# A fused attention and feed-forward kernel: the sixteen value products of a quad of heads issued in one block instead of two halves

## The chip, the cores and the metric

The kernel runs on one core of one Trainium2 chip. The metric is the device time of one execution in microseconds (us). The core has a matrix engine (TensorE, in the profile PE, with its weight loads as PEld), VectorE (DVE), ScalarE (ACT), GpSimd (POOL) and SyncE (SP), which issues DMAs. Each engine runs its own instructions in the order in which they are written; semaphores tie the engines to each other. Matrix products land in PSUM, which has eight banks of 128 x 512 f32.

## The reference, cut to what matters

```python
x = L0_attn_x                                    # (16, 512, 128) f32
x = x + _layernorm(attention(_layernorm(x)))     # 16 heads of width 8, queries serve as keys
x = x + _layernorm(feed_forward(_layernorm(x)))

# attention
q = (x @ Wq.T + bq).reshape(B, S, 16, 8)
v = (x @ Wv.T + bv).reshape(B, S, 16, 8)
bits = (einsum('bshe,en->bshn', concat(q, 1), hyperplanes) >= 0)   # 6 bits: 64 buckets
same = bucket[:, :, :, None] == bucket[:, :, None, :]
scores = einsum('bhsd,bhtd->bhst', q, q) / sqrt(128)
attn = softmax(scores * (62 + same), axis=-1)
out = einsum('bhst,bhtd->bhsd', attn, v)

# feed_forward, ternary weights with a scale for each output
h = silu(lin(x, w1)) * lin(x, w2)                # 128 -> 512
h = gelu(lin(h, h1)); h = gelu(lin(h, h2))       # 512 -> 512 -> 512
return lin(h, w3)                                # 512 -> 128
```

## The kernel before, in words

The sixteen sequences are sixteen iterations (called batches here). The work of one batch is spread over several of them: while iteration i computes the attention scores of batch i, it also does the feed-forward layers of batch i - 1, the last steps of batch i - 2, and the projections of the batches to come. The first two iterations have less of that, the last two as well, and a finale written out by hand ends the program.

**Tiles.** A batch has 64 score tiles: tile k is head k // 4 and rows 128 (k % 4) to 128 (k % 4) + 127. For each tile TensorE makes one bf16 matmul of 128 x 512 into one of four PSUM banks (`scores`, L593; tile k uses bank k % 4). It waits until tile k - 4 has been taken from that bank. VectorE (`attend_tile`, from L926) waits for the scores of tile k, then makes the coefficients 62 or 63 of tile k + 1 (`coefficients`, L901), and then in one instruction multiplies tile k by its coefficients, writes the logits to SBUF and takes the row maxima (L951). So the wait for scores k stands ahead of the coefficients of tile k + 1. The logits lie in a ring of 48 tiles.

**Groups and quads.** Eight tiles (two heads) are a group. Their maxima are transposed by VectorE, sent to DRAM and read back broadcast to all partitions (max_row); GpSimd then subtracts (L1125, two instructions for each group) and ScalarE exponentiates (`exponential`, L1185, 128 x 1024 each, eight for each quad). Sixteen tiles (four heads) are a quad. Its value products (`weigh_values`, L615) are sixteen matmuls, each of a stationary operand of 128 x 32 (values and a column of ones, padded) and a moving operand of 128 x 512. The four heads of the quad use four column strips of the array and four partition strips of one bank, aux_bank; j counts the four blocks of 128 keys. Two quads make a pair: their products accumulate in aux_bank, ScalarE copies them (oT, L1206), TensorE transposes them back (L624), ScalarE inverts the sums (rden, L1216), and VectorE divides (att, L974).

**What sets the order.** There is no scheduler. An iteration has 256 steps, four for each tile, and tables of numbers say after which step a piece of work is written out on its engine: scores k stand at step 4k, ahead of everything else of that step. `PV_SLOTS` has the steps of the sixteen value products j = 0..3 of quads 0 to 3 (each number stands for the four matmuls of one j); a number over 256 means the next iteration. In the program of before, j = 0 and 1 stand at one step and j = 2 and 3 at a later one, with one or two scores in between. The first half waits until all but two of the exponentials of the quad are done (probs_done), the second half waits for the last two. Feed-forward matmuls (L711 and L725 the gate and up products, L739 and L750 the two hidden layers, L766 the output) stand at steps of their own in between. The up products share banks with earlier ones: the third of them waits for VectorE's second multiply (L1007). On ScalarE, feed-forward activations, normalisations (L1321 is that of the attention output, which waits for a bias that VectorE makes) and exponentials alternate in a fixed order.

**Names used below.** L593 scores; L615 value products; L624 transposes of the output; L901 coefficients; L951 logits and maxima; L974 division; L1007 multiply of gate and up; L1185 exponentials; L1206 copy oT; L1216 rden; L1321 normalisation of the attention output.

Of the kernel before, what the change touches and what calls it, by code (L numbers as in the profile page):

```python
# [78 lines left out]
OUTPUT_BANK = 2  # L79


PV_SLOTS = (140, 140, 144, 144, 208, 208, 216, 216, 272, 272, 280, 280, 336, 336, 344, 344)
COPY_SLOTS = (218, 345)
TRANSPOSE_SLOTS = (231, 353)
SUM_SLOTS = (225, 363)
# [74 lines left out]
def sandwich_kernel(nc, x, wqT, bq, wvT, bv, hyper_blocks, hyper_bias, w1T, w2T, h1T, h2T, scales, w3T, w3_s, out):  # L160
    ctx = ExitStack()
    with ctx:
# [216 lines left out]
        def batches_at(i, k, slot, attend, feed):  # L379

            if attend and k == slot:
                return [i]
            if feed and k == slot - STEPS:
                return [i - 1]
            return []
# [189 lines left out]
        def _(pe):  # L575
# [20 lines left out]
            def weigh_values(b, quad, j, query, project):  # L596

                if j == 0:
                    if quad == 0:
                        pe.wait_ge(v_added, b + 1)  # L600

                    if quad == 0 and project:
                        pe.wait_ge(v_added, b + 2)
                    elif quad == 2 and query:
                        pe.wait_ge(q_part_steps, 4 * (b + 3))
                    elif quad % 2 == 0 and (begun(b) or quad):
                        pe.wait_ge(att_done, b * PAIRS + quad // 2)

                    pe.wait_ge(probs_done, b * (TILES // 2) + (quad + 1) * QT // 2 - GROUP)
                if j == 2:  # L610
                    pe.wait_ge(probs_done, b * (TILES // 2) + (quad + 1) * QT // 2)
                values = v_pad[:, b % 2].rearrange("p r n -> p (r n)")
                for hh in range(4):
                    first = 2 * PAD_PITCH * j + (PAD_PITCH - HALF_W) * (quad % 2) + VW * (quad // 2 * 4 + hh)
                    last = nc.tensor.matmul(aux_bank[hh * VW:(hh + 1) * VW, :], values[:, first:first + VW],  # L615
                                            logits[:, ring(b, quad * QT + hh * ST + j), :], start=(j == 0 and quad % 2 == 0),
                                            stop=(j == ST - 1 and quad % 2 == 1))
                if j == ST - 1:
                    last.then_inc(pv_psum, 1)
# [152 lines left out]
            def iteration(i, query, project, attend, feed, finish):  # L772
# [7 lines left out]
                for k in range(STEPS):  # L780
# [3 lines left out]
                    for quad in range(QUADS):  # L784
                        for j in range(ST):
                            for b in batches_at(i, k, PV_SLOTS[quad * ST + j], attend, feed):
                                weigh_values(b, quad, j, query, project)
# [708 lines left out]
```

## Time and profile before

| | us |
|---|---|
| median of 3 runs | 1331.74 |
| lowest and highest | 1331.31 to 1335.26 |
| the profiled execution, its own time | 1333.48 |
| its span, from the first to the last instruction | 1331.7 |
| busy in the span: TensorE | 1223.8 |
| busy: VectorE | 1212.8 |
| busy: ScalarE | 1091.9 |
| busy: GpSimd | 1167.6 |

An engine's busy time is the time in which one of its instructions runs. In the timeline a row is an instruction or several merged ones, with start and duration; the idle time ahead of it and what ended that stand in brackets. Each f32 matmul is two instructions of TensorE in the trace, so a half quad is sixteen rows of L615 and a quad thirty-two. Matmuls overlap: the next may start before the one before has ended.

### The profile page before, as it was taken

The numbers are of one execution on the slowest core, as the hardware profiler recorded it, in microseconds if no ns is written. First come the engines' busy times: TensorE is split into PE (matmuls) and PEld (weight loads), VectorE is DVE, ScalarE is ACT, GpSimd is POOL, SyncE is SP. The second block draws the span as 40 slices with busy tenths as digits, with TensorE's granted clock in tenths as the row PEclk, the third lists the DMA queues.
The fourth block names the chain that finished last, engine by engine and source line by source line (L and its number), as shares of the span: only waits on it lengthen the run. The fifth ranks groups of instructions, "written<-read, shape, count | busy, mean of one in ns | idle before, by whom it ended". The sixth has DMA issues, their size and how long they took to land. (4 is left out here: it accounts for less than half of the span.)

```text
span 1331.7 us, 19972 instructions
## 1 busy us (share of the span) xinstructions
PE 1223.8 (92%) x5406; PEld 506.8 (38%) x5406; DVE 1212.8 (91%) x3800; ACT 1091.9 (82%) x1693; POOL 1167.6 (88%) x304
## 2 busy tenths in 40 slices
PE   4667799999999999999999999999999999999998
PEld 1211244334344434434343433434343443434344
DVE  4989999999999999999999999999999999999920
ACT  2255879979798998989798897979889897988964
POOL 2599999999999999999999999999999999999600
PEclk9777999999999999999999999999999999999999
DMA  3474445435444543545454445544444454455200
GB/s 90 143 207 121 128 126 144 125 105 160 132 138 119 154 125 99 158 133 154 116 148 132 121 130 140 144 125 134 132 128 122 140 144 126 125 140 124 72 1 16
DMA packets 89237, 167.13 MB, mean 126 GB/s; under 512 B 18082, under 2 KB 54052, under 8 KB 89124
## 3 DMA queue, kind: packets, MB, share of 16 engines
q1 hardware_dynamic: 89016, 165.56, 45.1%
q8 instruction: 43, 0.70, 0.2%
q14 instruction: 70, 0.57, 0.1%
q10 hardware_dynamic: 108, 0.30, 0.1%
HBM read 150.33 MB, written 15.47 MB: 125 GB/s over the span
## 5 line engine op out<-in xcount | busy, mean ns | idle before, releaser
L1125 POOL TENSOR_TENSOR logits<-max_row,logits 128x2048 f32<-128x2048 f32 x252 | 1139.2, 4560 | 72.9 <-DMA max_row<-max_scratch 72.5
L951 DVE CUSTOM_DVE_ANT_0 logits<-s_bank,coeff 128x512 f32<-128x512 f32 x1024 | 691.6, 676 | 0.0
L1185 ACT ACTIVATE logits<-logits 128x1024 f32<-128x1024 f32 x504 | 503.0, 1047 | 92.6 <-POOL logits L1125 92.1
L901 DVE TENSOR_SCALAR coeff<-brow,bcol 128x516 bf16<-128x516 bf16 x1024 | 486.0, 475 | 29.2 <-PE s_bank L593 27.3
L593 PE MATMUL s_bank<-mov_stack,stat_stack 128*128 128x512 bf16 x1024 | 346.3, 393 | 46.4 <-DVE rowmax L951 40.4
L615 PE MATMUL aux_bank<-logits,v_pad 128*32 128x512 f32 x2016 | 247.3, 609 | 12.5 <-ACT logits L1185 12.4
L750 PE MATMUL f_bank<-hid_b,h_sb 128*128 128x512 f32 x480 | 236.7, 595 | 0.9 <-ACT hid_b L1355 0.9
L739 PE MATMUL f_bank<-hid_a,h_sb 128*128 128x512 f32 x480 | 234.4, 592 | 0.0
L593 PEld LDWEIGHTS s_bank<-mov_stack,stat_stack 128*128 128x128 bf16 x1024 | 95.6, 98 | 340.1 <-DVE rowmax L951 206.1
L739 PEld LDWEIGHTS f_bank<-hid_a,h_sb 128*128 128x128 f32 x480 | 90.2, 190 | 72.7 <-issue 61.8
L750 PEld LDWEIGHTS f_bank<-hid_b,h_sb 128*128 128x128 f32 x480 | 88.7, 190 | 66.3 <-issue 54.9
L615 PEld LDWEIGHTS aux_bank<-logits,v_pad 128*32 128x32 f32 x2016 | 53.3, 110 | 148.7 <-issue 114.5
L951 DVE DVE_READ_ACCUMULATOR2_ANT rowmax<- 128x1 f32 x1024 | 83.7, 82 | 0.0
L711 PE MATMUL f_bank<-ynT,w_sb 128*128 128x512 f32 x120 | 62.2, 620 | 10.6 <-ACT hid_a L1349 5.1
L1355 ACT ACTIVATE hid_b<-f_bank,scales_sb 128x512 f32<-128x512 f32 x60 | 38.0, 684 | 33.6 <-PE f_bank L739 33.4
L766 PEld LDWEIGHTS f_bank<-w_sb,hid_a 128*128 128x128 f32 x480 | 59.2, 192 | 16.2 <-issue 12.2
L725 PE MATMUL f_bank<-ynT,w_sb 128*128 128x512 f32 x120 | 64.4, 618 | 0.0
L1132 POOL TENSOR_TENSOR ffn<-ffn,y 128x512 f32<-128x512 f32 x15 | 19.1, 1275 | 49.3 <-ACT ffn L1198 49.3
L766 PE MATMUL f_bank<-w_sb,hid_a 128*128 128x128 f32 x480 | 62.0, 278 | 0.0
L1007 DVE SCALAR_TENSOR_TENSOR hid_a<-f_bank,scales_sb,hid_a 128x512 f32<-128x512 f32 x60 | 44.7, 746 | 4.6 <-PE f_bank L725 4.6
L1349 ACT ACTIVATE hid_a<-f_bank,scales_sb 128x512 f32<-128x512 f32 x60 | 37.9, 684 | 2.1 <-PE f_bank L711 1.8
L1355 ACT ACT_TABLE_LOAD x30 | 38.5, 1283 | 0.5
(168 smaller groups left out, 994.9 us busy)
## 6 DMA issues: line engine op xcount, KB each, us to landing
max_row<-max_scratch SPq DMA_DIRECT2D x128, 512.0 KB, 3.9
brow<-bucket_scratch SPq DMA_DIRECT2D x63, 522.0 KB, 6.3
mov_stack<-q_scratch SPq DMA_DIRECT2D x192, 96.0 KB
stat_stack<-q_scratch SPq DMA_DIRECT2D x189, 96.0 KB
max_scratch<-rowmax_T SPq DMA_DIRECT2D x512, 1.0 KB
q_scratch<-q_parts SPq DMA_DIRECT2D x16, 384.0 KB, 4.7
x_in<-in_x SPq DMA_DIRECT2D x16, 256.0 KB, 3.0
q_scratch<-q_parts SPq DMA_DIRECT2D x16, 256.0 KB, 5.2
```

Of the source, the lines that this page charges most:

```text
L593: nc.tensor.matmul(tile_bank(k)[:], stat_stack[:, quad % 2, hh, t * P:(t + 1) * P], mov_stack[:, quad % 2, hh, :], start=True, stop=True). ...
L615: last = nc.tensor.matmul(aux_bank[hh * VW:(hh + 1) * VW, :], values[:, first:first + VW], logits[:, ring(b, quad * QT + hh * ST + j), :], ...
L711: nc.tensor.matmul(f_bank[GATE_BANKS[j]][:], w1_sb[:, col], ynT[:], start=True, stop=True).then_inc(w1_psum, 1)
L725: nc.tensor.matmul(f_bank[UP_BANKS[j]][:], w2_sb[:, col], ynT[:], start=True, stop=True).then_inc(w2_psum, 1)
L739: last = nc.tensor.matmul(f_bank[FIRST_HIDDEN_BANKS[j]][:], h1_sb[:, k, col], hid_a[:, k, :], start=(k == 0), stop=(k == HT - 1))
L750: last = nc.tensor.matmul(f_bank[SECOND_HIDDEN_BANKS[j]][:], h2_sb[:, k, col], hid_b[:, k, :], start=(k == 0), stop=(k == HT - 1))
L766: last = nc.tensor.matmul(f_bank[OUTPUT_BANK][:, t * P:(t + 1) * P], hid_a[:, j, t * P:(t + 1) * P], w3_sb[:, j, :], start=(j == 0), stop= ...
L901: nc.vector.tensor_scalar(coeff[:, k % 3, :].rearrange("p (r n) -> p r n", r=ROW_RUNS), brow[:, h // 4 % 2, h % 4, :, 0:RUN], bcol[:, b % ...
L951: nc.vector.tensor_tensor_reduce(out=logits[:, ring(b, k), :], in0=tile_bank(k)[:], in1=coeff[:, k % 3, 0:SEQ], scale=float(E) ** -0.5, sc ...
L1125: nc.gpsimd.tensor_tensor(tiles[:, :, t:t + 2], max_row[:, m % 2].unsqueeze(2).broadcast_to([P, GROUP, 2, SEQ]), tiles[:, :, t:t + 2], ALU ...
L1185: nc.scalar.activation(logits[:, first:first + 2, :], logits[:, first:first + 2, :], ACT.Exp, scale=-1.0).then_inc(probs_done, 1)
L1355: nc.scalar.activation(hid_b[:, j, :], f_bank[FIRST_HIDDEN_BANKS[j]][:], ACT.Gelu, scale=scales_sb[:, 2, j:j + 1]).then_inc(h1_done, 1)
```

## The change

Of the table of steps for the value products, sixteen numbers are replaced. Of quad 0, j = 2 and 3 move from step 144 to 140, so they follow j = 0 and 1 directly. Of the other three quads, the first half moves four steps (one tile) later and the second half four steps earlier: 208 and 216 become 212, 272 and 280 become 276, 336 and 344 become 340. The waits stay in front of the same products: the wait for the quad's last two exponentials stands ahead of j = 2, now inside the block. The orders of VectorE, ScalarE, GpSimd and SyncE are unchanged. Quads 2 and 3 of the last batch are written out by the finale and are as before.

```diff
-PV_SLOTS = (140, 140, 144, 144, 208, 208, 216, 216, 272, 272, 280, 280, 336, 336, 344, 344)
+PV_SLOTS = (140, 140, 140, 140, 212, 212, 212, 212, 276, 276, 276, 276, 340, 340, 340, 340)
```

TensorE, quad 3 of the batch before (steps 80 to 92 of an iteration; quad 2, steps 16 to 28, reads the same). s_bank0 takes scores 20, s_bank1 scores 21, s_bank2 scores 22, s_bank3 scores 23; x8 and x16 count products:

```order
 L750 MATMUL f_bank2<-hid_b,h2_sb 128x512 x2
 L593 MATMUL s_bank0<-mov_stack,stat_stack 128x512
-L615 MATMUL aux_bank<-logits,v_pad 32x512 x8
-L593 MATMUL s_bank1<-mov_stack,stat_stack 128x512
-L593 MATMUL s_bank2<-mov_stack,stat_stack 128x512
-L615 MATMUL aux_bank<-logits,v_pad 32x512 x8
+L593 MATMUL s_bank1<-mov_stack,stat_stack 128x512
+L615 MATMUL aux_bank<-logits,v_pad 32x512 x16
+L593 MATMUL s_bank2<-mov_stack,stat_stack 128x512
 L593 MATMUL s_bank3<-mov_stack,stat_stack 128x512
 L593 MATMUL s_bank0<-mov_stack,stat_stack 128x512
```

Scores 21 moved ahead of the first eight products, and scores 22 stand behind all sixteen.

TensorE, quad 0 (steps 136 to 146); s_bank3 takes scores 35, s_bank0 scores 36, s_bank1 scores 37, and L766 is the feed-forward output:

```order
 L750 MATMUL f_bank1<-hid_b,h2_sb 128x512
 L593 MATMUL s_bank3<-mov_stack,stat_stack 128x512
-L615 MATMUL aux_bank<-logits,v_pad 32x512 x8
-L593 MATMUL s_bank0<-mov_stack,stat_stack 128x512
-L615 MATMUL aux_bank<-logits,v_pad 32x512 x8
+L615 MATMUL aux_bank<-logits,v_pad 32x512 x16
+L593 MATMUL s_bank0<-mov_stack,stat_stack 128x512
 L766 MATMUL f_bank2<-w3_sb,hid_a 128x128 x4
 L593 MATMUL s_bank1<-mov_stack,stat_stack 128x512
```

Scores 36 moved from between the halves to behind them.

TensorE, quad 1 (steps 208 to 216); s_bank0 takes scores 52, s_bank1 scores 53, s_bank2 scores 54, L725 are up products and L739 the first hidden layer:

```order
 L725 MATMUL f_bank1<-ynT,w2_sb 128x512
 L593 MATMUL s_bank0<-mov_stack,stat_stack 128x512
-L615 MATMUL aux_bank<-logits,v_pad 32x512 x8
-L725 MATMUL f_bank1<-ynT,w2_sb 128x512
-L593 MATMUL s_bank1<-mov_stack,stat_stack 128x512
-L593 MATMUL s_bank2<-mov_stack,stat_stack 128x512
-L615 MATMUL aux_bank<-logits,v_pad 32x512 x8
+L725 MATMUL f_bank1<-ynT,w2_sb 128x512
+L593 MATMUL s_bank1<-mov_stack,stat_stack 128x512
+L615 MATMUL aux_bank<-logits,v_pad 32x512 x16
+L593 MATMUL s_bank2<-mov_stack,stat_stack 128x512
 L725 MATMUL f_bank2<-ynT,w2_sb 128x512
```

The third up product and scores 53 moved ahead of the value products, scores 54 behind them all.

## Rows read from the trace of the kernel before

**Rows 1.** Page; stretch of batch 7: busy PE, PEld, DVE, ACT, POOL, clock.

```profile
PE 1223.8 (92%) x5406; PEld 506.8 (38%) x5406; DVE 1212.8 (91%) x3800; ACT 1091.9 (82%) x1693; POOL 1167.6 (88%) x304
...
567.60:644.20 76.60, 73.77 (x338) 31.21 (x337) 74.62 (x237) 68.62 (x107) 74.70 (x19) 1.00 0.49 134
```

**Rows 2.** VectorE's waits (total, times, longest): whole span, tiles 18-25 of batches 7, 10.

```profile
DVE coeff L901 <- PE s_bank L593: 27.3, 63, 4.7
...
DVE coeff L901 <- PE s_bank L593: 0.3, 1, 0.3
...
DVE coeff L901 <- PE s_bank L593: 1.4, 1, 1.4
```

**Rows 3.** Timeline (start, duration) of TensorE at quad 0's first half, batch 7.

```profile
603.67 0.38 PE L593 MATMUL s_bank<-mov_stack,stat_stack 128*128 128x512 bf16 x1
...
604.43 0.61 PE L615 MATMUL aux_bank<-logits,v_pad 128*32 128x512 f32 x4
...
605.29 0.61 PE L615 MATMUL aux_bank<-logits,v_pad 128*32 128x512 f32 x4
605.84 0.39 PE L593 MATMUL s_bank<-mov_stack,stat_stack 128*128 128x512 bf16 x1
```

**Rows 4.** Timeline of TensorE, then VectorE, at quad 2 (tiles 0 to 7).

```profile
568.58 0.38 PE L593 MATMUL s_bank<-mov_stack,stat_stack 128*128 128x512 bf16 x1
...
573.14 0.60 PE L593 MATMUL s_bank<-mov_stack,stat_stack 128*128 128x512 bf16 x2
...
568.54 0.68 DVE L951 CUSTOM_DVE_ANT_0 logits<-s_bank,coeff 128x512 f32<-128x512 f32 x1
...
573.15 0.48 DVE L901 TENSOR_SCALAR coeff<-brow,bcol 128x516 bf16<-128x516 bf16 x1
```

**Rows 5.** Timeline at quad 3: TensorE, VectorE; last, TensorE waiting at scores 45.

```profile
586.26 0.38 PE L593 MATMUL s_bank<-mov_stack,stat_stack 128*128 128x512 bf16 x1
...
593.41 0.38 PE L593 MATMUL s_bank<-mov_stack,stat_stack 128*128 128x512 bf16 x1
...
590.37 0.47 DVE L901 TENSOR_SCALAR coeff<-brow,bcol 128x516 bf16<-128x516 bf16 x1
...
593.83 0.48 DVE L901 TENSOR_SCALAR coeff<-brow,bcol 128x516 bf16<-128x516 bf16 x1 [0.28 <-PE s_bank L593]
...
615.46 0.39 PE L593 MATMUL s_bank<-mov_stack,stat_stack 128*128 128x512 bf16 x1 [0.54 <-DVE rowmax L951]
```

**Rows 6.** Timeline behind quad 3: TensorE in batch 2, ScalarE in batch 7.

```profile
206.95 0.66 PE L624 MATMUL aux_bank<-ident,oT 128*128 128x128 f32 x4 [0.54 <-ACT oT L1206]
...
590.95 0.58 ACT L1206 COPY oT<-aux_bank 128x512 f32<-128x512 f32 x1 [0.70 <-PE aux_bank L615]
```

**Rows 7.** Timeline at quad 0: VectorE's coefficients 37, ScalarE's last exponentials of the quad.

```profile
608.89 0.44 DVE L901 TENSOR_SCALAR coeff<-brow,bcol 128x516 bf16<-128x516 bf16 x1
...
603.34 2.00 ACT L1185 ACTIVATE logits<-logits 128x1024 f32<-128x1024 f32 x2
```

**Rows 8.** Timeline at quad 1: VectorE; last, where ScalarE's unbroken chain begins.

```profile
624.08 0.74 DVE L1007 SCALAR_TENSOR_TENSOR hid_a<-f_bank,scales_sb,hid_a 128x512 f32<-128x512 f32 x1
...
629.76 0.47 DVE L901 TENSOR_SCALAR coeff<-brow,bcol 128x516 bf16<-128x516 bf16 x1
...
631.22 0.75 DVE L1007 SCALAR_TENSOR_TENSOR hid_a<-f_bank,scales_sb,hid_a 128x512 f32<-128x512 f32 x1 [0.38 <-PE f_bank L725]
632.29 0.48 DVE L901 TENSOR_SCALAR coeff<-brow,bcol 128x516 bf16<-128x516 bf16 x1 [0.32 <-PE s_bank L593]
...
634.83 0.42 DVE L974 TENSOR_TENSOR att<-aux_bank,rden 128x256 f32<-128x256 f32 x1 [0.35 <-ACT rden L1216]
...
601.31 1.61 ACT L1321 ACTIVATE f_bank<-att,att_bias,att_rstd 128x128 f32<-128x128 f32 x4 [0.31 <-DVE att_bias L1019]
```

**Rows 9.** Batch 1 at quad 2: the view of stretches, then VectorE's timeline.

```profile
107.40:110.60 3.20, 3.20 (x18) 0.59 (x18) 3.20 (x11) 0.00 (x0) 3.20 (x1) 0.56 0.41 111
...
112.23 0.47 DVE L901 TENSOR_SCALAR coeff<-brow,bcol 128x516 bf16<-128x516 bf16 x1
```

## The prediction, made before the changed kernel ran

> **What bounds the kernel now.** I read the page first, then the windows of single batches, then who waits for whom, then the timeline of TensorE and VectorE side by side. Times in us are from the span's start; batch 7 (567.6 to 644.2) is my model batch, and "scores n" is the L593 matmul of tile n of a batch (64 tiles each). Over the span TensorE, VectorE and GpSimd are each busy for about nine tenths [rows 1]. Inside a batch of 76.6 VectorE works 74.6, GpSimd 74.7 and TensorE 73.8, at full granted clock [rows 1]. So VectorE is the bound, with about 2 us of holes per batch, and TensorE is close behind. The holes are named by the waits: 27.3 us in 63 waits of the coefficients L901 for scores, and in a batch the single wait at scores 25 is 0.3 at its shortest and 1.4 at its longest [rows 2]. (For the twelve like batches 2 to 13 it is 1.1, 1.1, 1.2, 0.4, 0.3, 0.3, 0.3, 0.3, 1.4, 0.3, 1.2, 0.7; two of these rows are shown.)
>
> What couples the two engines is four PSUM banks. Scores n may start when L951 has emptied tile n-4, which a wait of L593 on VectorE shows (the last row of [rows 5]), about 0.06 after; VectorE needs scores n before coefficients n+1. A bare VectorE tile is 1.00 us long (from L951 of tile 1 at 568.54 to the end of that of tile 5 at 573.15 are four tiles and one L951 of 0.61) [rows 4]. So TensorE has 3.0 us from "may start" to "is needed", and a TensorE block between two scores that is longer than that makes VectorE wait, unless VectorE has other work there.
>
> **The length of a block.** Each product is two f32 instructions, four products run side by side, and a group of four instructions follows the one before by 0.43 (604.43 to 605.29 is two groups) [rows 3]. A half quad (16 instructions) costs 2.17 from the scores ahead of it (603.67) to those behind it (605.84) [rows 3]. The whole quad is then 2.17 + 4 x 0.43 = 3.89. Two halves cost 4.34 and part a pair of scores; whole, the same work with one plain scores step (0.22, from the pair of L593 at 573.14 that takes 0.60, less 0.38 for one of them [rows 4]) is 4.11. So TensorE saves 0.23 per quad, what it costs to enter and leave the four-column form once. 62 quads are merged (the last two are issued by the finale): 14 us less TensorE time, but 3.89 is longer than 3.0. The DMAs, the other engines' orders and all durations stay.
>
> The Trainium skill (TensorEngine Tiling (Array Packing), Key Properties) says that changing the tiling mode drains TensorE. The rows bear this out in kind. By that rule alone the change is a plain gain of some 14 us; the coupling above is what speaks against it. The sum below does not use this.
>
> **Place A, quad 2 (scores 4 to 8).** Before, the first half follows scores 4 at 568.58 [rows 4] and fills the time until scores 5 may go. Now scores 5 come first: they wait for L951 of tile 1 (568.54 + 0.68 = 569.22) + 0.06 = 569.28, and TensorE stands idle for 0.5. Scores 6 start at 569.28 + 3.89 = 573.17, land at +0.39 = 573.56, and VectorE sees them at 573.60. It wants them at 573.15 [rows 4]. **VectorE +0.45**, TensorE +0.24 behind the block (scores 7 at 573.38 against 573.14). The scores behind it had little spare, but VectorE slips by more than TensorE, so nothing more is lost.
>
> **Place B, quad 3 (scores 20 to 25).** Scores 20 at 586.26 + 0.24 = 586.50 [rows 5]; scores 21 at 586.72 (VectorE's freeing is due at about the same time); scores 22 at 590.61, seen at 591.04. VectorE wants them at 590.37 + 0.45 = 590.82 [rows 5]: **+0.22**, together 0.67. TensorE is back on its old time (+0.24 - 0.23). Today VectorE waits 0.28 for scores 25 (593.41, used at 593.83) [rows 5]; arriving 0.67 later, it no longer does. **Net +0.39** in a batch whose wait there is 0.28. In general the slip is 0.67 less that wait, not below nothing. Where the wait is long it is not TensorE's own queue but L624 waiting for ScalarE's copy oT (206.95, idle 0.54) [rows 6], which hangs on GpSimd and stands still when VectorE slips. In batch 7 that copy waits for this block instead (590.95, 0.70) [rows 6] and comes 0.2 earlier, of no use.
>
> **Place C, quad 0 (scores 35 to 37).** Scores 36 move from 605.84 to 603.96 + 3.89 = 607.85 (scores 35 slip 0.29), seen at 608.28. VectorE wants them at 608.89 + 0.38, since statistics lie in between [rows 7]: **nothing**, the cover is 1.0.
>
> **Place D, quad 1 (scores 52 to 56).** Today TensorE waits 1.0 before the first half. Now L725 is ahead of it and waits as long for the multiply L1007 (624.08 + 0.74 = 624.82) [rows 8]. Scores 53 then at 624.88 + 0.86 = 625.74, in time (today VectorE waits 0.28 for them). Scores 54 at 629.63, seen at 630.06; wanted at 629.76 - 0.28 = 629.48: 0.58 late. The multiply that now waits 0.38 for L725 does not wait. Scores 55 at 629.63 + 0.22 + 1.72 = 631.57 (today 631.88), used at 631.99 against 632.29 [rows 8]: 0.3 gained. But next on VectorE is the division L974, which already waits 0.35 for ScalarE's rden (634.83) [rows 8]. ScalarE has no hole between L1321 (601.31, released by VectorE) and that rden [rows 8], and it has slipped with VectorE before. So the 0.3 becomes a longer wait at L974, about 0.65: **nothing kept**.
>
> **Sum of the twelve like batches.** 0.39 in the five whose wait is 0.3 (6, 7, 8, 9, 11), 0.3 in batch 5, nothing in 2, 3, 4, 10, 12, 13: 5 x 0.39 + 0.3 = **2.3**. Bounds: 0.39 less 12 x 0.3 if D's gain stays (-1.3), and 12 x 0.45 if GpSimd's lateness moves along with VectorE (+5.4).
>
> **Opening, batch 1.** Here TensorE is not loaded, starts A after an idle stretch, and the half quad runs at the lower clock level: 107.40 to 110.60 has a granted clock of 0.56 [rows 9], and TensorE is at the half quad for all of its 3.2. The whole quad behind scores 5 (108.06) then lasts about 5, scores 6 are seen at about 113.5 and wanted at 112.23 less today's 0.22 [rows 9]: +1.3. B likewise, estimated +0.9. At D (full clock) scores 54 and 55 come 0.55 and 0.28 late, where nothing is late today, and L974 does not wait: +0.8. Together **3.0**, between 0.9 (A and B at full clock) and 4.5. In batch 0 VectorE waits for ScalarE behind the blocks for longer than they cost: 0. **Batches 14 and 15** have less VectorE work beside the blocks (larger stalls in B) and get the waits of today back at scores 10, 23 and 25: between 0 and 0.8 each, I take 0.5: **1.0**.
>
> Sum: 2.3 + 3.0 + 1.0 = **+6.3**. The profiled execution took 1333.48 with a span of 1331.7; it lies 1.7 above the median of the runs, 1331.74. The sum would make it 1339.8, and the median 1331.74 + 6.3 = **1338.0**.
>
> **Rivals.** (1) The slips are swallowed. GpSimd is as full as VectorE [rows 1]; where its lateness sets scores 25 nothing is lost, and D's 0.3 may stay if ScalarE is early. 12 x 0.3 = 3.6 off the sum: 1334.4, within the noise. For it: half the batches show it now. Against: ScalarE's unbroken chain at D. Chance 0.25. (2) It is faster: what the denser products save TensorE is worth more than the long block costs. This holds if A and B don't stall, that is if a block really takes under 3.4 from scores to scores; then the waits at scores 25, 53, 55 and L1007 (0.28 + 0.28 + 0.32 + 0.38 = 1.26) fall by some half, 12 x 0.6 = 7 us: 1325. Against: 3.89 is counted from measured groups. Chance 0.09. The drain rule's own result, TensorE as the bound and 62 x 0.23 = 14 us less, gives 1317.5; VectorE's 74.6 of work per batch allows 2 us at most per batch, so chance 0.02. (3) Much slower: the wait for the quad's last exponentials now stands in mid-block with scores queued behind it. At C ScalarE is done at 603.34 + 2.00 [rows 7] + 0.38 = 605.72, and TensorE comes to the second half at 603.96 + 0.31 + 4 x 0.43 = 605.99, a margin of 0.3; the scores behind have 1.0 more, so it decides once ScalarE is over 1.3 late, or if at B GpSimd's late batches hold the block. At 0.5 per batch more: 12 x 0.5 on top, 1344. Chance 0.07. That the change does nothing is excluded by the order shown.
>
> **Numbers.** Forecast 0.57, rivals as above. A measurement tells about 0.3% (4.0 us) from no change, so slower begins at 1335.7. The forecast case falls below that bound at times (its own bounds reach from +1 to +11). Slower 0.61, same 0.28, faster 0.11. Range 1331 to 1343: it takes in rival 1 and most of the forecast's bounds.
>
> **What would show it.** L615 busy time falls by some 2 x 0.1 per quad. VectorE's waits on scores shift: none at 25 in most batches, new ones of 0.45 at scores 6, 0.2 at 22, 0.55 at 54, none at 53. TensorE gets a wait of 0.5 on VectorE before scores 5. L974's wait grows from 0.35 to about 0.65, sixteen times. Like batches are 77.0 or 77.5 long. If L974's wait does not grow, rival 1 is right; if scores 6 come in time, rival 2; a wait for exponentials inside L615 speaks for rival 3. The weakest terms are the opening and how GpSimd's lateness falls among the batches.

## The result, and the profile after

| | before | changed |
|---|---|---|
| median | 1331.74 | 1338.74 |
| lowest and highest | 1331.31 to 1335.26 | 1337.73 to 1340.93 |
| the profiled execution, its own time | 1333.48 | 1337.73 |
| its span | 1331.7 | 1335.9 |

The ratio is 1.0049, with a 95% interval of 1.0033 to 1.0066: the change makes the kernel slower, by 7 us in the medians. The medians are those of five runs of each. The profiled execution of the changed kernel is its fastest run, so the two profiles are only 4.2 us apart.

First the page of the changed kernel, the row that answers to [rows 1], and three of its groups (busy, mean ns of one, idle time ahead and what ended it):

```profile
PE 1215.8 (91%) x5406; PEld 516.6 (39%) x5406; DVE 1212.6 (91%) x3800; ACT 1091.3 (82%) x1693; POOL 1167.5 (87%) x304
...
L901 DVE TENSOR_SCALAR coeff<-brow,bcol 128x516 bf16<-128x516 bf16 x1024 | 486.7, 475 | 37.8 <-PE s_bank L593 35.7
...
L615 PE MATMUL aux_bank<-logits,v_pad 128*32 128x512 f32 x2016 | 234.8, 607 | 0.0
...
L725 PE MATMUL f_bank<-ynT,w_sb 128*128 128x512 f32 x120 | 62.8, 605 | 16.0 <-DVE hid_a L1007 16.0
```

TensorE is busy 8.0 us less (1223.8 in [rows 1]), and VectorE's waits for scores are 8.4 longer (27.3 in [rows 2], now 35.7). VectorE does the same work as before (1212.8 and 1212.6). TensorE's saving became idle time of TensorE and waiting time of VectorE.

Where in a batch this happens is shown by batch 7 of the changed kernel (572.1 to 649.0). Place A, TensorE, then VectorE; it answers to [rows 4]:

```profile
573.77 0.39 PE L593 MATMUL s_bank<-mov_stack,stat_stack 128*128 128x512 bf16 x1 [0.33 <-DVE rowmax L951]
574.09 3.64 PE L615 MATMUL aux_bank<-logits,v_pad 128*32 128x512 f32 x32
577.66 0.61 PE L593 MATMUL s_bank<-mov_stack,stat_stack 128*128 128x512 bf16 x2
...
577.63 0.08 DVE L951 DVE_READ_ACCUMULATOR2_ANT rowmax<- 128x1 f32 x1
578.09 0.48 DVE L901 TENSOR_SCALAR coeff<-brow,bcol 128x516 bf16<-128x516 bf16 x1 [0.38 <-PE s_bank L593]
```

TensorE waits for a bank ahead of scores 5, scores 6 start 3.89 us behind scores 5 (573.77 to 577.66), and VectorE, which has finished tile 5 at 577.71, waits 0.38. Place B and place D on VectorE, against [rows 5] and [rows 8]:

```profile
595.57 0.48 DVE L901 TENSOR_SCALAR coeff<-brow,bcol 128x516 bf16<-128x516 bf16 x1 [0.17 <-PE s_bank L593]
...
634.92 0.48 DVE L901 TENSOR_SCALAR coeff<-brow,bcol 128x516 bf16<-128x516 bf16 x1 [0.61 <-PE s_bank L593]
...
636.85 0.48 DVE L901 TENSOR_SCALAR coeff<-brow,bcol 128x516 bf16<-128x516 bf16 x1 [0.18 <-PE s_bank L593]
...
639.58 0.42 DVE L974 TENSOR_TENSOR att<-aux_bank,rden 128x256 f32<-128x256 f32 x1 [0.55 <-ACT rden L1216]
```

New waits stand at scores 22 and 54; that at scores 25 is gone, that at 55 is smaller, the multiply does not wait for L725, and the division waits 0.55 where it waited 0.35.

VectorE's waits, added up (total, times, longest), first in batch 1 and then in batches 2 to 13. Before:

```profile
DVE coeff L901 <- PE s_bank L593: 0.8, 3, 0.3
...
DVE coeff L901 <- PE s_bank L593: 18.0, 48, 1.4
DVE hid_a L1007 <- PE f_bank L725: 4.6, 12, 0.4
DVE att L974 <- ACT rden L1216: 4.2, 12, 0.4
```

After:

```profile
DVE coeff L901 <- PE s_bank L593: 5.1, 4, 2.4
...
DVE coeff L901 <- PE s_bank L593: 20.0, 63, 0.6
DVE att L974 <- ACT rden L1216: 6.7, 12, 0.6
```

In batches 2 to 13 the sum is the same in these two executions: 18.0 + 4.6 + 4.2 = 26.8 before, 20.0 + 6.7 = 26.7 after. In batch 1 it grew from 0.8 to 5.1. The batches' lengths say so too, taken from one L951 of tile 0 to the next (batch 15: to the end of its last L951): batch 1 75.3 and 80.1; batches 14 and 15 together 147.6 and 148.5; batches 2 to 13 together 924.9 and 924.6. But the last pair hides two movements. The shortest like batch grew from 76.63 to 76.91; and GpSimd's late batches, over 77.4 long and five of the twelve before, are one of twelve after.

What makes a batch late can be read from GpSimd's timeline. It is busy for 73.6 to 73.8 in every like batch of both kernels; what differs is when the DMA that brings the maxima back lets it go on, early in the batch. Batch 9 of before (from 720.9 on, 76.6 long) and batch 10 (from 797.5 on, 77.8 long):

```profile
727.69 4.54 POOL L1125 TENSOR_TENSOR logits<-max_row,logits 128x2048 f32<-128x2048 f32 x1 [1.34 <-DMA max_row<-max_scratch]
...
806.95 4.54 POOL L1125 TENSOR_TENSOR logits<-max_row,logits 128x2048 f32<-128x2048 f32 x1 [2.40 <-DMA max_row<-max_scratch]
```

It goes on 6.8 and 9.5 into the batch. Before, the batches in which this comes at 8.4 or earlier are 76.6 to 76.7 long, but for one of 77.6 in which a second wait for the same DMA follows; from 8.7 on they are 77.1 to 77.8. After, they are 76.9 up to 8.6, and 77.2 to 77.5 from 8.9 on. Four batches of before came later than 9.0 and none of after, so part of the second movement is how late this DMA was in each execution.

The end moved as well: from the last L951 to the end of the span it is 77.6 before and 76.7 after. In the traces of all kernels with quad 1 not in halves in the last batches it is 76.6 to 77.0, in all others 77.4 to 77.8.

### The profile page after: what moved, and what is told of

It reads as the page before. It is cut to its first block and busy times, and to the rows that moved or that the text cites. A ratio compares the mean times of both kernels' runs of the same rounds, so it can differ in the third digit from the quotient of the medians.

```text
span 1335.9 us, 19972 instructions
## 1 busy us (share of the span) xinstructions
PE 1215.8 (91%) x5406; PEld 516.6 (39%) x5406; DVE 1212.6 (91%) x3800; ACT 1091.3 (82%) x1693; POOL 1167.5 (87%) x304
## 5 line engine op out<-in xcount | busy, mean ns | idle before, releaser
L1125 POOL TENSOR_TENSOR logits<-max_row,logits 128x2048 f32<-128x2048 f32 x252 | 1139.1, 4553 | 77.1 <-DMA max_row<-max_scratch 73.7
L951 DVE CUSTOM_DVE_ANT_0 logits<-s_bank,coeff 128x512 f32<-128x512 f32 x1024 | 692.3, 676 | 0.0
L901 DVE TENSOR_SCALAR coeff<-brow,bcol 128x516 bf16<-128x516 bf16 x1024 | 486.7, 475 | 37.8 <-PE s_bank L593 35.7
L593 PE MATMUL s_bank<-mov_stack,stat_stack 128*128 128x512 bf16 x1024 | 350.0, 396 | 52.2 <-DVE rowmax L951 46.4
L615 PE MATMUL aux_bank<-logits,v_pad 128*32 128x512 f32 x2016 | 234.8, 607 | 0.0
L739 PE MATMUL f_bank<-hid_a,h_sb 128*128 128x512 f32 x480 | 234.4, 592 | 0.0
L593 PEld LDWEIGHTS s_bank<-mov_stack,stat_stack 128*128 128x128 bf16 x1024 | 98.3, 99 | 348.0 <-DVE rowmax L951 199.6
L739 PEld LDWEIGHTS f_bank<-hid_a,h_sb 128*128 128x128 f32 x480 | 90.2, 190 | 72.7 <-issue 61.7
L615 PEld LDWEIGHTS aux_bank<-logits,v_pad 128*32 128x32 f32 x2016 | 59.7, 111 | 146.7 <-issue 121.1
L951 DVE DVE_READ_ACCUMULATOR2_ANT rowmax<- 128x1 f32 x1024 | 84.3, 82 | 0.0
L725 PE MATMUL f_bank<-ynT,w_sb 128*128 128x512 f32 x120 | 62.8, 605 | 16.0 <-DVE hid_a L1007 16.0
L766 PEld LDWEIGHTS f_bank<-w_sb,hid_a 128*128 128x128 f32 x480 | 60.5, 192 | 4.8 <-issue 0.5
L766 PE MATMUL f_bank<-w_sb,hid_a 128*128 128x128 f32 x480 | 60.5, 275 | 0.0
```

Of the source, the lines that this page charges most:

```text
L593: nc.tensor.matmul(tile_bank(k)[:], stat_stack[:, quad % 2, hh, t * P:(t + 1) * P], mov_stack[:, quad % 2, hh, :], start=True, stop=True). ...
L725: nc.tensor.matmul(f_bank[UP_BANKS[j]][:], w2_sb[:, col], ynT[:], start=True, stop=True).then_inc(w2_psum, 1)
L739: last = nc.tensor.matmul(f_bank[FIRST_HIDDEN_BANKS[j]][:], h1_sb[:, k, col], hid_a[:, k, :], start=(k == 0), stop=(k == HT - 1))
L766: last = nc.tensor.matmul(f_bank[OUTPUT_BANK][:, t * P:(t + 1) * P], hid_a[:, j, t * P:(t + 1) * P], w3_sb[:, j, :], start=(j == 0), stop= ...
L901: nc.vector.tensor_scalar(coeff[:, k % 3, :].rearrange("p (r n) -> p r n", r=ROW_RUNS), brow[:, h // 4 % 2, h % 4, :, 0:RUN], bcol[:, b % ...
L951: nc.vector.tensor_tensor_reduce(out=logits[:, ring(b, k), :], in0=tile_bank(k)[:], in1=coeff[:, k % 3, 0:SEQ], scale=float(E) ** -0.5, sc ...
```

## The experiments

"Like batches" are batches 2 to 13. Medians of before in these three sets of runs were 1333.1, 1333.1 and 1332.5, so each kernel is judged by its ratio. Where a matmul's record is missing from a trace, the view writes "remote" for the releaser.

### Each quad alone

Four kernels, each with one row of the table changed, here quad 2:

```diff
-PV_SLOTS = (140, 140, 144, 144, 208, 208, 216, 216, 272, 272, 280, 280, 336, 336, 344, 344)
+PV_SLOTS = (140, 140, 144, 144, 208, 208, 216, 216, 276, 276, 276, 276, 336, 336, 344, 344)
```

Quad 0 alone (140 for all four j):

> Only quad 0 is issued whole (its second half moves from step 144 to 140); quads 1 to 3 stay in halves. Theory (a block costs only where it is longer than what the four banks let TensorE run ahead): scores 36 come 2.0 us later but VectorE has statistics there and 1.0 us to spare, so no new wait at scores 36 and no change: 1331.7 plus or minus 1. Rival (TensorE's time is the bound, and each merged block returns 0.23 us): sixteen times 0.23, some 3.5 us faster, 1328.

Measured 1333.03, ratio 1.0000 (0.9987 to 1.0013). No wait at scores 36 of a like batch, the shortest of which are 76.63 to 76.65 as before. The rival, TensorE's time as the bound, would be at 0.997 and is excluded.

Quad 1 alone (212):

> Only quad 1 is issued whole (step 212). Theory: in a full batch VectorE waits about 0.6 at scores 54 and 0.2 at scores 55 instead of 0.28 at 53, 0.38 at the multiply and 0.32 at 55; the 0.2 us won are lost again at the division, whose wait for ScalarE grows from 0.35 to 0.56. So nothing in batches 2 to 13, +0.8 in batch 1, +0.5 in batch 15: 1331.7 + 1.4 = 1333.1. Rival (the gain is kept): 12 x 0.2 less, 1330.7, with a division wait of 0.35 as before.

Measured 1334.52, ratio 1.0008 (0.9996 to 1.0019), as expected but not clear of nothing. What decides is the trace, VectorE's waits in the like batches:

```profile
DVE coeff L901 <- remote: 15.8, 24, 2.3
DVE att L974 <- ACT rden L1216: 6.9, 12, 0.6
```

The multiply's 4.6 is gone and the division's 4.2 has become 6.9 with only this quad changed; the shortest like batch is 76.63. The gain at D is made and given back within the batch.

Quad 2 alone (276):

> Only quad 2 is issued whole (step 276, place A). Theory: 0.38 us of new wait at scores 6; TensorE comes out 0.24 later, so the wait at scores 25 falls only by 0.14 where it was 0.28, and a full batch gets 0.24 longer; where GpSimd's lateness set scores 25, nothing. Batch 1 pays 1.6 (lower clock). Sum 6 x 0.24 + 1.6 = 3.0: 1334.7. Rival (loss spread evenly, a price for every whole block): a quarter of the 7.0, 1333.5, with the like batches paying it.

Measured 1338.17, ratio 1.0035 (1.0022 to 1.0049): by the medians the larger part of the whole loss in this one place, and 4.7 us where 3.0 were expected. The shortest like batch is 76.94, 0.3 longer (0.24 expected). In the opening its block took 5.91 and VectorE waited 2.9 for scores 6; batch 1 is 2.4 longer, more than the 1.6 expected. This profile's span is 5.9 longer than that of before: 1.4 of it lie in the like batches and 2.4 in batch 1, but 2.6 were there when batch 1 began, and up to there the two programs are the same. So a profile of the opening holds differences of some 2 us that no change made, and how much of the 4.7 the opening's block is worth stays open here. An even price of 1.0012 per quad is excluded.

Quad 3 alone (340):

> Only quad 3 is issued whole (step 340, place B). Theory: 0.4 us of new wait at scores 22, and the wait of 0.28 at scores 25 goes away, as TensorE is 0.23 earlier and VectorE 0.4 later: +0.1 in a full batch, +1.8 in batch 1 (lower clock), +0.3 in each of batches 14 and 15: 1331.7 + 3.5 = 1335.2. Rival (even price): 1333.5.

Measured 1332.76, ratio 1.0001 (0.9990 to 1.0013), where 1.0026 was expected: a miss. The wait at scores 22 is 0.33 and that at 25 gone, so a like batch stays at 76.61. Batch 1 does wait 2.1 for scores 22, but that replaces three waits and later slack: the batch is 76.7, 1.5 longer, not 1.8. And batches 14 and 15 are 0.6 shorter together, where 0.6 longer was expected. The wait of 0.72 at scores 22 replaces 0.19 + 0.41, which costs 0.1 in each; batch 14 comes out as long as before, and in batch 15 a wait of VectorE for ScalarE (L1019, 0.21) is gone and the division's fell from 0.35 to 0.19. The rest of batch 15's gain stays open.

### The opening

In iterations 0 and 1 halves, later whole blocks:

```diff
+EARLY_PV_SLOTS = (140, 140, 144, 144, 208, 208, 216, 216, 272, 272, 280, 280, 336, 336, 344, 344)
...
-                            for b in batches_at(i, k, PV_SLOTS[quad * ST + j], attend, feed):
+                            for b in batches_at(i, k, (EARLY_PV_SLOTS if i < 2 else PV_SLOTS)[quad * ST + j], attend, feed):
```

> As the changed kernel, but in iterations 0 and 1 the value products keep their halves; whole blocks from iteration 2 on. In the profiles batch 1 took 80.1 us against 75.3 before, and all batches from 2 on together only 0.6 us more. Theory (the loss is the opening's, where a whole block starts after an idle stretch at the lower clock level): 4.9 us less than the changed kernel, 1333.8, batch 1 back at 75.3. Rival (batch 1 only takes a slip that later batches would take instead, GpSimd being the real bound): 1337 to 1339.

And the reverse, whole blocks in iterations 0 and 1 only:

> The reverse: whole blocks only in iterations 0 and 1, halves from iteration 2 on. Theory: the opening's loss alone, 1331.7 + 4.9 = 1336.6, batch 1 at 80.1 us. Rival: the slip is swallowed by the waits of later batches, 1332 to 1333.

Measured 1335.10, ratio 1.0016 (1.0002 to 1.0030), and 1337.68, ratio 1.0028 (1.0014 to 1.0041). They add up to 1.0044, the changed kernel's loss within the intervals. So by the medians the opening is the larger part, some 3.7 us, and the other fourteen batches give some 2, though the two intervals overlap. Batch 1 is 75.2 with halves and 80.3 with whole blocks. (The profile of the second kernel is its slowest run; it begins batch 1 at 108.4, the changed kernel at 106.0, with the same program up to there.) The rival, by which later batches swallow the opening's slip, is excluded.

Why the opening costs so much is seen at its blocks of 32 instructions. The stretch of the first one of batch 1 in the reverse kernel and those of both in the changed kernel (length, busy PE, PEld, DVE, ACT, POOL, granted clock, DMA), and the timeline of the two blocks in the changed kernel:

```profile
110.70:116.80 6.10, 6.10 (x33) 1.33 (x34) 3.38 (x11) 2.00 (x2) 6.10 (x2) 0.58 0.91 229
...
108.30:113.10 4.80, 4.80 (x34) 1.07 (x33) 3.38 (x11) 2.00 (x2) 4.80 (x2) 0.74 0.86 226
127.20:132.80 5.60, 5.60 (x34) 1.23 (x34) 3.62 (x15) 2.00 (x2) 5.60 (x2) 0.63 0.75 206
```

```profile
106.74 0.39 PE L593 MATMUL s_bank<-mov_stack,stat_stack 128*128 128x512 bf16 x1 [3.39 <-DVE rowmax L951]
107.74 0.61 PE L593 MATMUL s_bank<-mov_stack,stat_stack 128*128 128x512 bf16 x1 [0.61 <-DVE rowmax L951]
108.28 4.88 PE L615 MATMUL aux_bank<-logits,v_pad 128*32 128x512 f32 x32
113.09 1.04 PE L593 MATMUL s_bank<-mov_stack,stat_stack 128*128 128x512 bf16 x4
...
126.62 0.61 PE L593 MATMUL s_bank<-mov_stack,stat_stack 128*128 128x512 bf16 x1 [0.39 <-DVE rowmax L951]
127.16 5.68 PE L615 MATMUL aux_bank<-logits,v_pad 128*32 128x512 f32 x32
```

TensorE had been idle between the scores ahead of each (3.39 and 0.61 ahead of the first, 0.39 in the row ahead of the second). The blocks take 4.88 and 5.68 instead of 3.64, since they begin at the lower clock level (0.5 of 2.4 GHz) and end at the upper: the mean of 0.58 above is nearly all of it at the lower. Length times mean granted clock is about the same for all of them: 6.18 x 0.58, 4.88 x 0.74 and 5.68 x 0.63 are 3.58 to 3.61, and at the upper level the block takes 3.64. So the clock accounts for the whole of the extra length. VectorE waits 1.84 and 2.37. (The Trainium skill, TensorE: Matmul & The Clock Gate, Part 1, has the lower level as the state after idleness. The first block's rows agree; ahead of the second the idle stretches are short, 0.33 to 0.70 between the scores from 115 on but for one of 1.38, and the level is the lower one all the same.)

To take the clock away and leave the block, unneeded matmuls fill TensorE's idle time ahead of both blocks:

```diff
                         scores(i, k // STEPS_PER_TILE)
+                        if feed and not finish and 4 <= k <= 80 and k != 20:
+                            nc.tensor.matmul(f_bank[2][:, 0:384], ident[:], h1_sb[:, 0, 0:384], start=True, stop=True)
```

> The changed kernel with one unneeded matmul (f32, 384 columns, into an unused bank) behind each of scores 1 to 4 and 6 to 20 of iteration 1, where TensorE was idle between the scores and its blocks ran at the lower clock level (4.9 and 5.7 us instead of 3.6). Theory (the opening's loss is the lower clock, not the block alone): blocks of 3.6 us, VectorE's waits at scores 6 and 22 of batch 1 fall from 1.84 and 2.37 to about 0.4 each, batch 1 from 80.1 to about 77, 3 us less: 1335.7. Rival (the block waits there for exponentials that GpSimd's lateness delays): blocks as long as before, 1338.7 or more.

Both blocks of this kernel in TensorE's timeline, and VectorE's waits in its batch 1 (L903 is L901 there):

```profile
109.17 3.64 PE L615 MATMUL aux_bank<-logits,v_pad 128*32 128x512 f32 x32
...
126.60 3.64 PE L615 MATMUL aux_bank<-logits,v_pad 128*32 128x512 f32 x32
...
DVE coeff L903 <- remote: 1.0, 2, 0.7
DVE att_bias L1021 <- ACT f_bank L1295: 0.5, 1, 0.5
DVE coeff L903 <- PE s_bank L593: 0.2, 1, 0.2
```

The waits at scores 6 and 22 are 0.38 and 0.11, and batch 1 is 76.6 instead of 80.1 (75.3 before): the clock is the cause of 3.5 of the 4.9 us that batch 1 lost in the profiles, and the rest is there with blocks at full clock. The median, 1337.19, ratio 1.0035 (1.0021 to 1.0049), fell less than the 3 us expected. The intervals of the two kernels overlap, so in the times the gain is not shown, and what the rest of the runs lost elsewhere their times don't tell.

### The length of a block

The products split twelve and four, the four a tile later:

```diff
-PV_SLOTS = (140, 140, 144, 144, 208, 208, 216, 216, 272, 272, 280, 280, 336, 336, 344, 344)
+PV_SLOTS = (140, 140, 140, 144, 212, 212, 212, 216, 276, 276, 276, 280, 340, 340, 340, 344)
```

> Each quad in a block of twelve products (at 140, 212, 276, 340) and one of four a tile later. TensorE's time is that of before (two blocks for each quad), but the long block takes 3.03 us from scores to scores, just what the banks allow. Theory (3.0 us decide): no wait of VectorE at scores 6 and at most 0.1 at scores 22, where the changed kernel has 0.38 and 0.17; TensorE comes out of quads 2 and 3 about 0.5 late, so scores 25 wait up to 0.8, and a full batch is 0.3 to 0.5 longer than before where that wait was 0.28. About 1336. Rival (VectorE waits because of the idle stretch ahead of the block, not its length): waits at scores 6 of 0.3 or more stay.

TensorE's timeline at place A, batch 7:

```profile
573.24 0.39 PE L593 MATMUL s_bank<-mov_stack,stat_stack 128*128 128x512 bf16 x1 [0.33 <-DVE rowmax L951]
573.55 2.78 PE L615 MATMUL aux_bank<-logits,v_pad 128*32 128x512 f32 x24
576.27 0.39 PE L593 MATMUL s_bank<-mov_stack,stat_stack 128*128 128x512 bf16 x1
576.59 1.07 PE L615 MATMUL aux_bank<-logits,v_pad 128*32 128x512 f32 x8
```

The idle stretch of 0.33 ahead of the block is still there; from scores 5 to scores 6 are 3.03 us; and in none of the like batches does VectorE wait for scores 6 or 22. So length decides, and not the idle stretch. Where the limit lies the runs tell too, and it is not 3.0. At place A the whole block's 3.89 from scores 5 to scores 6 gave a wait of 0.38, and the slow one in the opening 5.35 (107.74 to 113.09) gave 1.84: both leave 3.51. Here scores 6 were there at 576.70 (576.27 + 0.39 + 0.04), and VectorE finished tile 5 at 577.17, so 3.03 left 0.47 to spare, which is 3.50 again. That is four tiles of 1.00, less 0.06 from VectorE's end to TensorE's start, 0.39 for the scores and 0.04 until VectorE has them. As a version it is worse: 1340.67, ratio 1.0055 (1.0038 to 1.0072), a like batch at least 77.13. TensorE saves nothing and still idles ahead of the blocks, which VectorE feels later, above all at the multiply:

```profile
DVE hid_a L1007 <- PE f_bank L725: 9.4, 12, 0.8
```

That is 0.8 in each batch against 0.4 before. The time expected, 1336, left this out.

### Where quad 1's gain goes

First the division a tile later, on VectorE alone:

```diff
-DIVIDE_SLOTS = (224, 364)
+DIVIDE_SLOTS = (228, 364)
```

> The changed kernel with the first division of a batch one tile later on VectorE (step 228 instead of 224). Theory: its wait for ScalarE's rden, 0.56 us in each of batches 2 to 13, is gone and with it the place where quad 1's gain is given back: up to 12 x 0.56 = 6.7 us less, 1332. TensorE's transposes at step 240 need that division and may come up to 0.6 later, so 1332 to 1335. Rival (something behind it, GpSimd or the q parts on ScalarE, takes the slip in its place): 1338.7 plus or minus 1, with longer waits of VectorE at L988 or of TensorE at L637.

The rival was right: median 1339.51, ratio 1.0042 (1.0026 to 1.0059), a like batch still 76.9. The division waits no more, and VectorE's waits in the like batches have a new row instead:

```profile
DVE aux_bank L988 <- ACT qT L1244: 6.3, 12, 0.5
```

TensorE's transposes of the input of the batch after next (L637) use the division's bank and wait for it, and that batch's query hangs on them: delaying a step only passes its wait on. The second attempt brings the operand earlier:

```diff
-COPY_SLOTS = (218, 345)
-TRANSPOSE_SLOTS = (231, 353)
-SUM_SLOTS = (225, 363)
+COPY_SLOTS = (214, 345)
+TRANSPOSE_SLOTS = (227, 353)
+SUM_SLOTS = (219, 363)
```

> The changed kernel with the first pair's copy oT on ScalarE ahead of two exponentials (step 214 instead of 218), its transposes on TensorE at 227 instead of 231 and the sums on ScalarE at 219 instead of 225: the division, left in its place, then finds its operand ready. Theory (at the division the gain of quad 1 is given back): the wait at L974 goes from 0.56 to 0 and, since the transposes behind it come earlier too, nothing takes its place: a like batch of 76.35 instead of 76.91, 12 x 0.56 = 6.7 us less, 1332. Rival (as with the division moved later, another wait takes it: L988 or GpSimd): 1338 to 1339.

Measured 1332.31, ratio 1.0001 (0.9991 to 1.0012), a like batch 76.29: no wait at the division, none at L988, and 0.6 per batch shorter, as expected. The same on top of the kernel before:

> The kernel before with the same three steps moved (copy 214, transposes 227, sums 219). Its second half of quad 1 ends at 630.1 in the model batch, just before the copy would start. Theory: the division's wait of 0.35 goes, a like batch is 76.28 instead of 76.63, 4.2 us less: 1327.5 to 1329 (beside 1331.7 to 1333.1 for the kernel before). Rival: no change.

Measured 1329.33, ratio 0.9970 (0.9958 to 0.9982), a like batch 76.42 where 76.28 was expected: the wait at scores 25 grew from 0.28 to 0.41.

### A version that beats both

Halves in iterations 0 and 1 and for quad 2, whole blocks otherwise, and the three earlier steps:

```diff
+PV_SLOTS = (140, 140, 140, 140, 212, 212, 212, 212, 272, 272, 280, 280, 340, 340, 340, 340)
+EARLY_PV_SLOTS = (140, 140, 144, 144, 208, 208, 216, 216, 272, 272, 280, 280, 336, 336, 344, 344)
```

> A version meant to beat both: halves in iterations 0 and 1 and for quad 2 throughout, whole blocks for quads 0, 1 and 3 from iteration 2 on, and the three earlier steps. Theory: no wait at scores 6, 0.33 at 22, none at 25 in most batches, 0.6 and 0.18 at 54 and 55 with the won 0.2 kept, none at the division: a like batch of 76.61 - 0.57 = 76.05, some 7 us less than the kernel before: 1325. Rival (whole blocks cost as such): no better than the halves with the same three steps, 1328 or more.

Measured 1326.83, ratio 0.9963 (0.9949 to 0.9978), a like batch 76.17. In batches 2 to 13 its VectorE waits for nothing but scores (L902 is L901 there):

```profile
DVE coeff L902 <- PE s_bank L594: 10.7, 35, 0.5
DVE coeff L902 <- remote: 8.3, 14, 0.8
```

That is 19.0 against 26.8 before. It is faster than the kernel before and than the changed one. It fell short of the 76.05 and the 1325 expected. That it beats the halves with the same three steps is seen in the like batch (76.17 against 76.42), not in the times, whose intervals overlap. The wait at scores 22 is 0.47, not 0.33.

## Why the prediction was right, point by point

The forecast was 1338.0 and the median is 1338.74. Direction, mechanism and total were right; two of its terms were mis-sized, in opposite directions, and a third was left out, so that the total is only 0.7 off is in part luck.

**The bound and the coupling.** The bound is right: quad 0 alone shows that 0.23 us less TensorE time per quad is worth nothing. The coupling is right in kind, but its general sentence (3.0 us from "may start" to "is needed") is not what decides: the block stands behind scores 5, which may go a tile earlier than scores 6, so VectorE waits only for what is over 3.51 us from scores 5 to scores 6. The working of place A and rival 2 go by 3.44 and 3.4, not by the 3.0, and so the sum did not suffer.

**The block.** 3.89 from scores to scores, as worked out from the groups of four. L615 is busy 12.5 less over the page (247.3 before, 234.8 after), 0.2 per quad; TensorE as a whole is busy 8.0 less, not 14.

**The places.** Worked out and measured: A 0.45 and 0.38; B 0.22 and 0.17; C nothing and nothing; D 0.58 and 0.61 at scores 54, at 55 0.28, its figure for the opening, and 0.18; the idle stretch ahead of scores 5 0.5 and 0.33; the division's wait "about 0.65" in sixteen batches and 0.55 in twelve; the wait at 25 gone in eight of the twelve like batches, and at most 0.4 in the others. A and B were each some 0.06 too large because I took the start of the coefficients' row as the time at which VectorE wants scores; it is still reading the accumulator for 0.07 then (577.63 + 0.08 above). So a like batch whose wait at 25 had been 0.28 grew by 0.28, not 0.39.

**The twelve like batches.** Predicted +2.3, measured -0.4 in the profiled pair. The step that failed took GpSimd's late batches as given: five late before, one after. Over the shortest like batch the twelve had 924.9 - 12 x 76.63 = 5.3 us before and 924.6 - 12 x 76.91 = 1.7 after; in the profiles of the other kernels with all four quads whole in these batches this excess was between 1.1 and 4.4, and in those of the two others with all four in halves 3.2 and 6.2. It differs from execution to execution with the DMA that GpSimd waits for, and no run here ties how many batches are late to the change. That a late batch gets no longer the prediction had right. Of the 2.7 between its +2.3 and the -0.4, 0.6 are the 0.11 too much in each of five batches; the other 2.1, an estimate by what is left, are batches that happened not to be late. In the medians, whole blocks from iteration 2 on cost 2.1 (0.3 to 4.0), where the prediction has 2.3 + 1.0. Whether a longer VectorE path makes late batches rarer, as a mean over many executions, stays open.

**The opening.** Predicted +3.0 (0.9 to 4.5), measured +4.9 in batch 1. The mechanism, the lower clock, is shown by the filled opening. The mis-sized term is the block's length there: taken as about 5 from scores to scores at A and less at B, it was 5.35 and 6.14 (blocks of 4.88 and 5.68), with blocks of 5.9 and 6.2 in other kernels, as the clock rises at another point of the block each time. Outside the profiled pair the opening is worth some 3.7 in the medians.

**Batches 14 and 15, and the end.** Predicted +1.0, measured +0.51 and +0.44. The end behind the last tile, for which the prediction has no term, became 0.9 shorter; the traces tie this to quad 1 (above), and why is not shown.

**The rivals.** (1) was the nearest: its first part is real, since a late batch is as long as its lateness makes it in both kernels (GpSimd going on at 9.1 gave 77.4 before, at 9.0 it gave 77.3 after); its second falls, as the quad-1 kernel shows that D's gain is not kept. It would have given a kernel slower by less than 0.3%. (2) falls with quad 0. (3) did not occur: L615 has no wait ahead of it on the page after (0.0).

**The range.** The prediction says that its own bounds reach from +1 to +11. Its three terms' bounds add up to -0.4 (-1.3 + 0.9 + 0) and +11.5 (5.4 + 4.5 + 1.6). The range given, 1331 to 1343, is about that wide, and nothing else rests on it.

## What to carry to other kernels

With n banks between a producer and a consumer, and a producer that fills each bank as soon as it is free, the consumer waits for what a block between two fills takes beyond n consumer tiles, less the hand-overs both ways and the fill itself (here 4 x 1.00 - 0.49 = 3.51 from fill to fill), however much time the block saves. Only n = 4 was run here; for another n this is argued. Move such a block to where the consumer has other work, as at quad 0. Read a gain through to the next fixed meeting point of the engines: delaying the waiting step passed the wait on, bringing its operand earlier removed it. And look at the opening apart: the block that made VectorE wait 0.38 in the full pipeline ran there at half the clock for a part of its length, and the wait was 1.84.

## What the runs showed of the hardware that was not expected

One and the same block of 32 matmuls took 3.64, 4.88, 5.68, 5.91 and 6.18 us, by where in it the granted clock rose; matmuls of no use ahead of it brought it to 3.64 both times. Entering and leaving the four-column form once costs 0.23 us of TensorE time for blocks of 8, 16, 24 and 32 instructions alike: from scores to scores they take 1.32, 2.17, 3.03 and 3.89, which is 0.43 for each four instructions and 0.45 besides, 0.22 of it a plain scores step. In the profiles of these kernels GpSimd's late batches added between 1.1 us (the filled opening) and 6.2 us (whole blocks in the opening only) to the twelve like batches, a spread of 5 us beside the 7 of the change.
